# One core: an attention block and a GRU over 16 sequences, with the features of the projections' contraction in another order over the partitions

## The reference, cut to what matters

```python
scale, shift = split(cond @ W_emb + b_emb)              # per batch, 512 each
xn  = rms_norm(x, g_norm) * (1.0 + scale) + shift
q, k, v = split(xn @ W_qkv)                             # W_qkv: 512 x 1536, 16 heads of 32
q, k = rms_norm(q, g_q), rms_norm(k, g_k)               # over the 32 of a head
o   = softmax(q @ k.T * 32 ** -0.5) @ v
x   = x + (o + o @ W_out)
hs  = GRU over the 256 steps of x, initial state cond, W_ih and W_hh 512 x 1536
out = x + hs
```

## Time and profile before

| what | value |
|---|---|
| median of 3 runs | 1692.28 us (1691.51 to 1694.1) |
| the profiled execution's own time | 1693.31 us |
| its span, first to last instruction | 1691.7 us |
| PE busy in it | 1662.7 us (98%) |
| DVE, ACT, POOL busy | 1172.5, 960.9, 419.1 us (69%, 57%, 25%) |
| mean granted TensorE clock | 0.998 of full speed |

### The profile page before, as it was taken

The page is one execution under the profiler, slowest core; times in us unless marked ns, Lnnn a source line. Parts: engine busy times, 40 slices in busy tenths (PEclk is TensorE's granted clock), DMA queues, the critical chain, the costliest instruction groups (busy, mean ns, idle before and its releaser), DMA issues.

```text
span 1691.7 us, 68248 instructions
## 1 busy us (share of the span) xinstructions
PE 1662.7 (98%) x28505; PEld 1222.8 (72%) x28505; DVE 1172.5 (69%) x4108; ACT 960.9 (57%) x3521; POOL 419.1 (25%) x477
## 2 busy tenths in 40 slices
PE   9999999999999998999999999999999999999996
PEld 7787788878787876666666666766666666666664
DVE  5888888878888875466666666666666666666665
ACT  5777777777777774344444444444444444444444
POOL 3544444444444432011111111111111111111111
PEclk9999999999999999999999999999999999999999
DMA  7244433334433326434433433434434334334331
GB/s 238 52 124 119 113 89 91 98 96 100 100 89 88 88 79 157 104 79 81 84 75 78 87 76 78 82 75 79 82 73 87 77 75 84 75 78 87 70 68 25
DMA packets 302027, 151.38 MB, mean 89 GB/s; under 512 B 142780, under 2 KB 281224, under 8 KB 301720
## 3 DMA queue, kind: packets, MB, share of 16 engines
q1 hardware_dynamic: 300272, 146.40, 39.1%
q10 hardware_dynamic: 1448, 0.61, 0.1%
HBM read 84.61 MB, written 62.13 MB: 87 GB/s over the span
## 4 chain that ended last, share of the span: by engine, by line
PE 94%; DVE 2%; ACT 1%; DMA 1%; POOL 1%; issue 1%; SPq 0%; DVEq 0%; POOLq 0%
PE ps L828 39%; PE ps L799 20%; PE ps L561 14%; PE ps L640 7%; PE ps L676 5%; PE ps L621 4%; PE ps L655 4%; PE ps L663 1%; DMA wstage<-in_L_cond_W_qkv_dram 1%; POOL rq L1503 1%; PE ps L600 0%; PE ps L582 0%; ACT P L1309 0%; DVE nmx L936 0%; DVE v L1153 0%
## 5 line engine op out<-in xcount | busy, mean ns | idle before, releaser
L828 PE MATMUL ps<-whh,hT 128*32 128x192 f32 x16384 | 712.9, 326 | 11.9 <-DVE hT L1179 11.9
L828 PEld LDWEIGHTS ps<-whh,hT 128*32 128x32 f32 x16384 | 495.9, 110 | 210.0 <-DVE hT L1179 81.0
L1434 ACT ACTIVATE v<-ps 128x128 f32<-128x128 f32 x512 | 139.0, 272 | 433.6 <-PE ps L828 433.6
L799 PE MATMUL ps<-wih,x1T 128*32 128x256 f32 x6144 | 378.2, 380 | 0.7 <-ACT x1T L1328 0.7
L1568 POOL TENSOR_TENSOR outG<-hG,GI 128x128 f32<-128x128 f32 x255 | 116.9, 459 | 902.8 <-DVE hG L1172 902.8
L1153 DVE SCALAR_TENSOR_TENSOR v<-v,ps 128x64 f32<-128x64 f32 x512 | 113.2, 221 | 275.2 <-ACT v L1434 275.2
L799 PEld LDWEIGHTS ps<-wih,x1T 128*32 128x32 f32 x6144 | 199.6, 110 | 108.3 <-issue 2.2
L1309 ACT ACTIVATE P<-ps,nmx 128x256 f32<-128x256 f32 x496 | 229.1, 482 | 0.3 <-DVE nmx L936 0.3
L1442 ACT ACTIVATE v<-v 128x64 f32<-128x64 f32 x512 | 131.1, 256 | 106.8 <-DVE v L1158 106.5
L1503 POOL TENSOR_TENSOR rq<-msq,mh 128x16 f32<-128x16 f32 x64 | 185.9, 2905 | 5.3
L936 DVE TENSOR_REDUCE nmx<-ps 128x4 f32<-128x1024 f32 x128 | 156.1, 1219 | 18.3 <-PE ps L621 18.3
(11 more groups left out here) (136 smaller groups left out, 1956.8 us busy)
## 6 DMA issues: line engine op xcount, KB each, us to landing
gscr<-nat SPq DMA_DIRECT2D x96, 256.0 KB, 3.0
GI<-gscr SPq DMA_DIRECT2D x124, 192.0 KB, 4.8
xres<-in_x_dram SPq DMA_DIRECT2D x32, 256.0 KB, 3.4
xscr<-x1s SPq DMA_DIRECT2D x32, 256.0 KB, 2.7
xblk<-x1s SPq DMA_DIRECT2D x128, 64.0 KB, 2.7
GI<-xscr SPq DMA_DIRECT2D x128, 64.0 KB, 2.5
x1n<-xblk SPq DMA_DIRECT2D x124, 64.0 KB, 2.4
out_dram<-outG SPq DMA_DIRECT2D x124, 64.0 KB, 2.2
```

Of the source, the lines that this page charges most:

```text
L799: last = pe.matmul(F[G % 2][q, n], x1T[:, tt % 2, j, c, :], wih[:, c, g * D + 256 * half:g * D + 256 * half + 256], start=(c == 0), stop=( ...
L828: last = pe.matmul(ps[32 * j:32 * j + 32, q, 0:192], hT[:, 32 * c:32 * c + 32], whg[:, c, :, 128 * j + 64 * q:128 * j + 64 * q + 64], star ...
L1434: s.activation(v_rz[:, q, :], ps[:, q, 64:192], ACT.Tanh, scale=0.5).then_inc(s_tr, 1)
```

## The change

Feature 128a + 32c + k now lies in chunk c at partition 32a + k. Then a group `a` of 32 partitions needs 128 features that are next to each other in DRAM, and one DMA for each group does: `load_x` issues 4 DMAs for a batch, with pieces of 512 bytes. Each part of `W_qkv` comes by 4 DMAs instead of one, because a DMA's partition side has one step: each fills 32 partitions with 4 rows of 2 KB. The scaled rows of batch 0 and 1 are written with their features in the new order, into `sq` and `raw` and not in place; the copies of `cond`'s projection are written in that order too, and `b_emb` and `g_norm` come as three DMAs in place of two. Since `raw` now holds rows of batch 1 until PE has turned them, `normalize` waits for that before its first write. The counts of the semaphores follow.

```diff
                 for a in range(4):
-                    for c in range(KC):
-                        f = 128 * c + 32 * a
-                        sp.dma_start(xq[32 * a:32 * a + 32, :].rearrange("p (r c k) -> p r c k", r=8, c=KC)[:, :, c, :],
-                                     x[b, :, f:f + 32].rearrange("(r t) k -> t r k", r=8)).then_inc(s_x, 16)
+                    sp.dma_start(xq[32 * a:32 * a + 32, :].rearrange("p (r f) -> p r f", r=8),
+                                 x[b, :, 128 * a:128 * a + 128].rearrange("(r t) f -> t r f", r=8)).then_inc(s_x, 16)
...
             def load_w(g):
-                sp.dma_start(wstage[:, :, g * D:(g + 1) * D],
-                             W_qkv[:, g * D:(g + 1) * D].rearrange("(c p) n -> p c n", p=128)).then_inc(s_lw[g], 16)
+                for a in range(4):
+                    sp.dma_start(wstage[32 * a:32 * a + 32, :, g * D:(g + 1) * D],
+                                 W_qkv[128 * a:128 * a + 128, g * D:(g + 1) * D].rearrange("(c k) n -> k c n", c=KC)).then_inc(s_lw[g], 16)
...
                         c = 2 * half + k
-                        rows = V[:, 0] if b == 1 else xb
+                        rows = raw if b else sq
...
-            pe.wait_ge(s_lc, 64)
+            pe.wait_ge(s_lc, 80)
...
-                rows = V[:, 0] if b == 1 else xb
+                rows, scaled = (V[:, 0], raw) if b else (xb, sq)
                 for i in range(2):
-                    v.tensor_scalar(rows[:, i, :], rows[:, i, :], rx[:, i:i + 1], None, ALU.mult).then_inc(s_xs, 1)
+                    v.tensor_scalar(scaled[:, i, :].rearrange("p (c a k) -> p a c k", a=4, c=KC),
+                                    rows[:, i, :].rearrange("p (a c k) -> p a c k", a=4, c=KC), rx[:, i:i + 1], None,
+                                    ALU.mult).then_inc(s_xs, 1)
...
                 v.wait_ge(s_rq, 2 * k + 2)
+                if k == 0:
+
+                    v.wait_ge(s_xT, 4)
...
-            v.tensor_copy(V[:, 1, 0, :], ps[:, 4, :]).then_inc(s_cd, 1)
+            v.tensor_copy(V[:, 1, 0, :].rearrange("p (c a k) -> p a c k", a=4, c=KC),
+                          ps[:, 4, :].rearrange("p (a c k) -> p a c k", a=4, c=KC)).then_inc(s_cd, 1)
...
-                s.wait_ge(s_lw[g], 16)
+                s.wait_ge(s_lw[g], 64)
...
-            s.dma_start(vnat[0:8, :], b_emb.rearrange("(c p) -> c p", p=128)).then_inc(s_lc, 16)
-            s.dma_start(vnat[8:12, :], g_norm.rearrange("(c p) -> c p", p=128)).then_inc(s_lc, 16)
+            for k, u in enumerate((b_emb[0:D], b_emb[D:2 * D], g_norm)):
+                s.dma_start(vnat[4 * k:4 * k + 4, :].rearrange("c (a k) -> c a k", a=4),
+                            u.rearrange("(a c k) -> c a k", a=4, c=KC)).then_inc(s_lc, 16)
```

More of the change, by code:

```diff
@@ L1218, in square_blocks @@
             def square_blocks(m):
-                s.wait_ge(s_x, 16 + 256 * (m - 1))
+                s.wait_ge(s_x, 16 + 64 * (m - 1))
                 if m == 2:
@@ L1350, in _ @@
             s.wait_ge(s_cp, 2)
-            s.copy(V[:, 1, 1, :], ps[:, 5, :]).then_inc(s_ca, 1)
+            s.copy(V[:, 1, 1, :].rearrange("p (c a k) -> p a c k", a=4, c=KC),
+                   ps[:, 5, :].rearrange("p (a c k) -> p a c k", a=4, c=KC)).then_inc(s_ca, 1)
             wq_high(1, 0, 1)
```

## The result

| | kernel before | changed kernel |
|---|---|---|
| median | 1692.44 us (9 runs) | 1698.15 us (9 runs, 1696.1 to 1702.24) |
| ratio | | 1.0033, 95% interval 1.0025 to 1.0041 |
| the profiled execution's own time | 1693.31 us | 1702.24 us |
| its span | 1691.7 us | 1700.4 us |

The change costs 5.7 us, 0.34%. The forecast was +2.4 us, a range to 1697.0, and 0.17 for "slower". The direction of the mechanism was right, its size was not, and the time lies above the range.

A forecast was written before the change was run, and what follows sets the result against it. It took gapless PE to bound attention and the k part's landing to bound the start. The k part's +2.4 us, all other terms 0, on the median 1692.28 gave 1694.7 us, range 1691.8 to 1697.0.

The forecast's parts named there:

- What bounds the kernel: PE without gaps bounds attention; the start hangs on the k part's landing, so its delay passes fully to the end.
- The k part by 4 DMAs: In the start, loads on 32 partitions run at 203 to 214 GB/s, landing at 16.4 us instead of 14.0: +2.4 us.
- Rival B: In the start, PE idles, its clock falls, and batch 0's products cost 1.1 us more: 1695.8 us, chance 0.15.
- Sum: All terms together: +2.4 us, 1694.7 us against the median 1692.28, chance 0.62.
- The q part's cover: In the start, the q part lands at 22.9 us and may come 1.1 us later before it costs: 0.
- x by 4 DMAs: Loads of x per batch: 12 issues fewer for each of 14 batches; PE never waited on them: gain 0.
- `x_scale`: Scaling of batches 0 and 1 in the start, new order with runs of 32: 0, at most 0.4 us.
- the third small DMA: On ACT's queue in the start: may move the table load and first squares by 0.3 us, inside 1.3 us of cover.
- the new wait: In `normalize`, for PE's transposes of batch 1: 2.7 us of cover, so 0.
- C: Rival on the x loads: ACT's 9.7 us of waiting for x is on the path and won back: 1685.0 us, chance 0.04.
- A: Rival on the k part's load: the quarters run at full rate, nothing lands later: 1692.3 us, chance 0.15.

The follow-up runs named there:

- e11_rest: The changed kernel with each part of `W_qkv` loaded by one whole-width DMA as before: 1693.3 us against 1693.0, ratio 1.0001.
- e4_fill: The changed kernel with 22 more filling transposes on PE ahead of the first product (36 for 14): 1699.86 us against 1693.26, ratio 1.0038.
- e6_order: The changed kernel with the four quarters of each part of `W_qkv` issued in the order 0, 2, 1, 3: 1697.44 us against 1693.0, ratio 1.0028.
- e8_four_whole: The kernel before with each part of `W_qkv` by 4 DMAs over all 128 partitions: 1693.08 us against 1692.58, ratio 1.0004.
- e2_narrow_w: The kernel before with only each part of `W_qkv` by 4 DMAs of 32 partitions: 1699.07 us against 1693.26, ratio 1.0034.
- e9_after_wemb: The changed kernel, but SP issues the k part only after all of `W_emb` has landed: 1698.73 us against 1692.58, ratio 1.0031.
- e7_wait_k: The changed kernel, but SP waits until the k part has landed before issuing what follows: 1698.09 us against 1693.0, ratio 1.0036.
- order3: Another profiled execution of e6_order, nothing changed against it: own time 1700.86 us.
- order2: Another profiled execution of e6_order, nothing changed against it: own time 1697.74 us.
- again2: Another profiled execution of the changed kernel, nothing changed against it: own time 1702.90 us.
- e5_narrow_qv: The kernel before with only the q and v parts by 4 narrow DMAs each: 1694.43 us against 1692.58, ratio 1.0007.
- e12_two_queues: The changed kernel with quarters 2 and 3 of each part of `W_qkv` issued from ACT's queue: 1697.78 us against 1693.0, ratio 1.0031.

## Why the prediction was right and wrong

- **What bounds the kernel: right.** Attention stayed gapless; the start hangs on the k part, and all of its delay passes (18.74 us from the first cast to the first scores in the kernel before, e11_rest, e4_fill and e6_order alike).
- **The k part by 4 DMAs: the step that failed.** The term was "+2.4 us", landing at 16.4 instead of 14.0, with a bound of 2.6. Measured from ACT's first cast it was +5.47 us in the profile beside the earlier trace rows, and +4.0 to +6.3 in the four of the changed kernel; only e4_fill's, +2.6, agrees. That narrow DMAs are the cause was forecast and is shown (e8_four_whole, e2_narrow_w), and their own rate was right: 213 GB/s in e9_after_wemb, where the k part comes alone. What was wrong is the sum: it has the k part alone at that rate, with `W_emb` done at 11.3 as before, and puts at nothing what the narrow DMAs do to the loads around them. But the DMA engines are not in step (e7_wait_k), so narrow and whole-width DMAs are in flight together. In this profile the rate was 135 GB/s while they were (10.5 to 13 us), lower than that of either kind alone, and `W_emb`'s last part came 2.5 us late.
- **The sum put right, as far as it goes.** From 10 us to the first cast the kernel before moved 397 GB/s over 4.03 us, 1.60 MB, and the changed one 188 over 9.50 us, 1.79 MB. The forecast halved the rate of 1.05 MB only. 1.6 MB at 203 GB/s take 7.9 us in place of 4.0, so +3.9 us, a little under the best of the four executions (+4.0). Of the other 1.6 us in this profile, 0.6 is the rate of 188 instead of 203 GB/s, pulled down by the stretch at 135, whose like no row of before showed; 1.0 is the 0.19 MB more that went ahead, at 188 GB/s.
- **Rival B, the clock: happened,** beside the forecast and not in its place. I gave it 0.15 and 1.1 us. It fell in all four executions of the changed kernel, after PE had been idle for 3.0 to 3.7 us, in order3 after 2.6 and in e7_wait_k after 2.5; in e6_order and order2, after 1.4 and 2.0 us, it stayed at 1.00. In the four it cost 0.93, 1.00, 2.12 and 1.00 us: again2 had it at 0.50 for twice as long. The price was right in three of them. The mistake was to price it as a rival to the forecast when a longer wait makes it likelier.
- **Sum:** in the four profiles the landing and the clock together make the first scores 5.0 to 8.5 us late, and the executions took 4.5 to 9.6 us longer than the profiled one before. The 5.7 us of the medians lie inside that.
- **The q part's cover: too large.** I had the q part at 22.9 us, with 1.1 us to spare. In the changed kernel ACT waited 1.04 us for it, until 27.2, and it cost nothing only because PE, slow by its clock, was later still; that is luck. In order2, with the clock at 1.00, it cost 0.24 us, in e5_narrow_qv some 0.6 and in e12_two_queues 1.45.
- **x by 4 DMAs, `x_scale`, the third small DMA, the new wait: nothing shown against 0.** Together they are 1.0001 (0.9992 to 1.0009) in e11_rest; one by one only `x_scale` was measured, 485 ns before and after. DMA packets fell from 302027 to 256510, and ACT's wait for x in the earlier trace rows is gone from the list of waits. So C falls: that wait was on no path. A falls with the profile after, where nothing ran at the full rate.

**Open:** what makes one execution run its narrow loads at 160 and another at 220 GB/s, and why the mixture of narrow and whole-width loads runs at 134 to 157 GB/s in some and at 215 in others. e7_wait_k shows that the DMA engines finish up to 2.5 us apart, but no row names single engines, so which of them lag, and whether more of them do in the slow executions, is not known.

## What to carry to other kernels

Look at how many partitions a DMA writes: from 10 to 14 us the kernels with the k part by four DMAs of 32 partitions behind `W_emb` on one queue had 160 to 251 GB/s, where the one with four of 128 had 395, and the number of DMAs cost nothing. When a layout is changed to merge the transfers that nobody waits for, look at what it does to the ones at the start that everybody waits for. And price a slower load with the DMAs around it in the queue, and with the clock that falls while PE waits.

## What the runs showed of the hardware that I had not expected

- Narrow DMAs slow the whole-width ones ahead of them: the last 512 KB of `W_emb` were waited for until 14.09 us, and not at all when the k part was issued behind their landing. With both kinds in flight full engines moved 135 GB/s in the profile after (134 to 215 in its like), where the narrow ones alone had 213 and the whole-width ones 395.
- One and the same program lands its k part anywhere from 18.07 to 20.36 us, and with only more filling on PE at 16.65.
- The DMA engines finish apart: with nothing behind the k part their share fell from 1.05 at 14 us to 0.35 and 0.16 before the end at 17 us.
- Narrow DMAs that follow each other in one queue are faster when they write different halves of the partitions: 238 and 241 GB/s against 210 to 218.
- Two queues with different halves of the partitions moved 279 GB/s from 10 us to the first cast, against 170 to 246 for one. The Trainium skill, SBUF — State Buffer, "Can I just issue two DMAs to hit both halves?", says that two such DMAs at once gave only 6% more. The 279 are 13% above the best of the five and 64% above the worst, but the stretches differ in what else was in flight, so this is no clean test of it.
